# Taps on column tiles of the array: two convolutions of a four-block vision kernel

## The chip, the cores and the metric

The kernel runs on one core of a Trainium2 chip. The metric is the device time of one execution in microseconds (us); the time before is the median of three runs. A core has five engines with their own instruction streams: TensorE (PE, with its weight loads listed as PEld), VectorE (DVE), ScalarE (ACT), GpSimd (POOL) and SyncE (SP), which here only issues transfers. They wait for each other by semaphores.

## The reference, cut to what matters

The input is 16 images of 96 channels and 16 x 16 pixels. Four blocks follow each other, and each is a mixer and a feed-forward, both on a normalised x and added to x.

```python
# mixer of block 0: every channel by itself
out = bn_l(dwconv(x, w_large, 13x13)) + bn_s(dwconv(x, w_small, 3x3)) + bn_i(x)
# mixer of block 1: linear projections, softmax attention of 6 heads
# mixer of block 2: v, q at full size, k, off at stride 2, all depthwise 3x3
value, query = dwconv(x, w_v) + b_v, dwconv(x, w_q) + b_q
key, off     = dwconv(x, w_k, stride 2) + b_k, dwconv(x, w_off1, stride 2) + b_off1
o   = gelu(layernorm(off) * ln_g + ln_b)
pos = tanh(o @ w_off2 + ref_points)
v_sampled = bilinear_sample(value, pos)             # 64 points an image
out = (query . key * scale) @ v_sampled             # 12 heads, no softmax
y   = out @ w_out
# mixer of block 3: depthwise 3x3 q, k, v, and an attention
# feed-forwards of blocks 0 to 2: four experts, two of them weighted for each pixel
h = gelu(x @ w1[e] + b1[e]);  y = sum over e of gate[e] * (h @ w2[e] + b2[e])
# feed-forward of block 3: sign weights; outputs scaled by the largest value of a group
z = bitlinear(x, W1, b1)   # 5 groups; clip(a * 128 / (max|a| + eps), +-(128 - eps))
h = gelu(z);  y = bitlinear(h, W2, b2)
```

## The kernel before

X lies in SBUF as 32 tiles of 128 pixels x 96 channels for the whole time, and each block adds to it. Everything is float32, and each float32 product is two PE instructions in the trace. Each of the eight parts is a function with one block of five engine streams, written out by hand in the order in which they run, with semaphores between them.

`l0_conv` (lines 208 to 407) takes 12 groups of 8 channels. A group's pixels are turned by two PE transposes (line 373) so that the 128 partitions are 8 channels x 16 columns x of the image; ScalarE copies them to `xt` (line 295). A row of taps r of the 13 is then one 128 x 128 band matrix, block diagonal over the channels, which ScalarE fills from `band` by eight strided copies for three groups at a time (`fill`, line 287). `conv_group` (line 388) adds 13 products into PSUM, each with the image rows that its shift leaves. `turn_back` (line 397) turns the result into pixels, and VectorE adds it to X (line 355). The BN factors are 36 powers on GpSimd (line 267), beside the two sets of 16 for the normalisation (line 272).

`moe` (lines 847 to 1129) is the expert feed-forward; the class `ExpertFront` (lines 457 to 550) holds its first steps, which for block 0 stand at the head of `moe`: statistics and root, apply, `pe_turn` (line 540), the copies to a high and a low part, the weight splits, `pe_gates` (line 547). The first product of the experts is at line 1081.

`l2_conv` takes eight pairs of images (`p`), and one pass of its loop holds the first half of pair p and the second half of pair p - 1. `third_xp` is the padded transposed image (96 channels on the partitions), double buffered. `conv` (line 1886) makes a depthwise 3x3 of nine products, each with a 96 x 96 diagonal matrix from `third_diag` and a shifted view. It serves the offsets (`conv_offsets`), the keys and the queries; the values are made by VectorE with nine taps (`value_taps`, line 1718; the first by ScalarE). `scores` (line 1936) multiplies queries and the keys that GpSimd spread over heads (`kb`, line 1650); `sample` (line 1947), `outputs` (line 1957) and `project` (line 1966) finish a pair. In `outputs` a product has 64 x 32 tiles at three column positions. The class `ThirdFront` makes the first normalised tiles and the diagonal inside the expert block before.

The order of TensorE in one pass:

```python
conv_offsets(p); project(p - 2, 1); scores(p - 1, 0); scores(p - 1, 1)
turn_offsets(p); conv_keys(p); turn_values(p - 1)
conv_queries(p, 0, 4); sample(p - 1, 0); turn_back(p)
conv_queries(p, 4, 7); sample(p - 1, 1); positions(p)
conv_queries(p, 7, TAPS); outputs(p - 1, 0); turn(p + 1)
outputs(p - 1, 1); project(p - 1, 0)
```

`l3_ffn` takes five groups of six tiles (768 pixels). For a group: `turn`, `ups` (three chunks of 512 pixels, then three of 256), the maximum over the whole group (`top_in`, `top_out`), `factors` and `clip` on VectorE (line 2483), `gelus` on ScalarE (line 2562), `downs` (line 2611), `results`, `add_results`. `add_term` (GpSimd, line 2407) and `scale_term` (ScalarE, line 2533) add the last value term of the attention to X, `rstd_of` (line 2412) makes the root in three batches, one group and one group and then two, and `stay_awake` (line 67) puts products of the identity with itself on TensorE.

## Time and profile before

| | us |
|---|---|
| median of three runs | 1257.62 |
| lowest and highest run | 1248.44, 1257.85 |
| profiled execution, its own time | 1257.45 |
| span of that execution in the trace | 1255.6 |
| granted TensorE clock, mean | 0.968 |

The span is the time from the first to the last recorded instruction; the profiled execution is 1.85 us longer. A clock of 1.00 is 2.4 GHz, and 0.5 is 1.2 GHz. A row of the timeline is a run of like instructions: its start, the time from the first start to the last end, engine, line, operation, tiles, count, and in brackets how long the engine had been idle and what it waited for. "PE" rows can overlap the next row, since the last instruction's end is counted in.

### The profile page before, as it was taken

The page shows a single profiled execution, that of the slowest core. Times are in us where ns is not written, and L with a number is a line of the kernel's source. Part 1 is how long each engine was busy: PE and PEld are TensorE (multiplying, and loading weights), DVE is VectorE, ACT ScalarE, POOL GpSimd, SP SyncE. Part 2 cuts the span into 40 slices and gives each one's busy share as a digit, 9 for nine tenths or more (in the row PEclk, how much of TensorE's full clock was granted, in tenths as well). Part 3 has the DMA queues.
Part 4 walks back from the last instruction along what each step waited for, and adds up shares of the span by engine and source line. Part 5 has one row for each costly group of instructions (what it writes and reads, how often), then busy time and mean ns, then how long its engine had stood idle before and what let it go on. Part 6 is the DMA issues. An engine that isn't in the chain of part 4 may idle for free. (4 is left out here: it accounts for less than half of the span.)

```text
span 1255.6 us, 24199 instructions
## 1 busy us (share of the span) xinstructions
PE 1170.9 (93%) x8554; PEld 1023.1 (81%) x8554; DVE 807.0 (64%) x2909; ACT 482.4 (38%) x942; POOL 255.6 (20%) x239
## 2 busy tenths in 40 slices
PE   1989999989999999999999999999999999999776
PEld 1978999978999998999997767678999987887555
DVE  6036767666766653778775656655877767776645
ACT  3614434325555553434342232233334322332542
POOL 4003121220110001321222422342121222111200
PEclk9998999998999998999999999999999999999786
DMA  3301001010000000000000000000000000000000
GB/s 137 88 2 66 23 1 49 1 51 1 1 2 1 2 1 1 2 1 0 0 1 1 2 1 2 1 1 1 2 1 0 0 1 1 1 1 4 1 10 38
DMA packets 11563, 15.70 MB, mean 13 GB/s; under 512 B 7385, under 2 KB 9007, under 8 KB 11346
## 3 DMA queue, kind: packets, MB, share of 16 engines
q1 hardware_dynamic: 10754, 12.86, 3.2%
q10 hardware_dynamic: 720, 1.66, 0.3%
q8 instruction: 55, 0.90, 0.3%
q14 instruction: 34, 0.28, 0.1%
HBM read 11.37 MB, written 3.15 MB: 12 GB/s over the span
## 5 line engine op out<-in xcount | busy, mean ns | idle before, releaser
L1091 PEld LDWEIGHTS moe_dn<-all_w,moe_hid 128*128 128x128 f32 x2304 | 269.8, 192 | 5.5
L1091 PE MATMUL moe_dn<-all_w,moe_hid 128*128 128x96 f32 x2304 | 271.8, 275 | 0.0
L1024 ACT ACTIVATE moe_hid<-moe_up 128x512 f32<-128x512 f32 x288 | 169.9, 598 | 232.3 <-PE moe_up L1083 219.3
L1081 PE MATMUL moe_up<-front_xh,front_w1h 97*128 97x512 f32 x288 | 122.4, 425 | 0.6 <-PEq L1141 0.3
L1083 PE MATMUL moe_up<-front_xl,front_w1h 97*128 97x512 f32 x288 | 114.4, 397 | 0.0
L1082 PE MATMUL moe_up<-front_xh,front_w1l 97*128 97x512 f32 x288 | 113.6, 394 | 0.0
L969 DVE SCALAR_TENSOR_TENSOR all_X<-moe_dn,front_gate,all_X 128x96 f32 (+1 forms) x384 | 95.4, 310 | 26.0 <-PE moe_dn L1091 20.3
L961 DVE SCALAR_TENSOR_TENSOR all_X<-all_b,front_gate,all_X 128x96 f32 (+1 forms) x384 | 100.9, 324 | 5.8 <-DVE front_var L83 2.8
L916 POOL TENSOR_TENSOR front_prob<-front_euler,front_logit 128x16 f32<-128x16 f32 x21 | 60.9, 2902 | 190.6 <-DVEq L424 190.6
L1477 PE MATMUL l1c_o<-second_vs,l1c_pt 128*128 128x64 f32 x768 | 92.8, 274 | 0.4 <-DVE l1c_ro L1287 0.4
L1477 PEld LDWEIGHTS l1c_o<-second_vs,l1c_pt 128*128 128x128 f32 x768 | 90.2, 192 | 2.8 <-issue 0.6
L1253 DVE TENSOR_REDUCE second_nmax<-l1c_sc 128x2 f32<-128x512 f32 x96 | 61.8, 686 | 37.6 <-PE l1c_sc L1446 36.6
L1718 DVE SCALAR_TENSOR_TENSOR l2c_val<-third_xp,all_l_taps,l2c_val 96x544 f32<-96x544 f32 x64 | 65.2, 1019 | 13.6 <-ACT l2c_val L1794 11.0
L2159 DVE SCALAR_TENSOR_TENSOR l3c_ykv<-fourth_xp,all_l_taps,l3c_ykv 96x256 f32<-96x256 f32 x128 | 65.1, 508 | 4.0
L1886 PE MATMUL l2c_qp<-third_xp,third_diag 96*96 96x512 f32 x144 | 65.8, 592 | 0.0
L1083 PEld LDWEIGHTS moe_up<-front_xl,front_w1h 97*128 97x128 f32 x288 | 54.7, 190 | 12.7
L2283 PE MATMUL l3c_qp<-fourth_xp,fourth_wqt 96*128 96x256 f32 x288 | 64.8, 378 | 0.0
L1376 ACT ACTIVATE l1c_pt<-l1c_st 128x512 f32<-128x512 f32 x96 | 52.1, 595 | 32.6 <-PE l1c_st L1462 31.5
L1081 PEld LDWEIGHTS moe_up<-front_xh,front_w1h 97*128 97x128 f32 x288 | 55.3, 192 | 9.4 <-issue 1.0
L1082 PEld LDWEIGHTS moe_up<-front_xh,front_w1l 97*128 97x128 f32 x288 | 55.3, 192 | 8.8
L2283 PEld LDWEIGHTS l3c_qp<-fourth_xp,fourth_wqt 96*128 96x128 f32 x288 | 53.2, 189 | 6.9
L388 PE MATMUL l0c_cp<-l0c_xt,l0c_full 128*128 128x176 f32 (+6 forms) x312 | 56.0, 336 | 0.0
(418 smaller groups left out, 2017.5 us busy)
## 6 DMA issues: line engine op xcount, KB each, us to landing
all_w<-w SPq DMA_DIRECT2D x3, 582.0 KB
all_w<-w SPq DMA_DIRECT2D x3, 576.0 KB
all_X<-x_rows SPq DMA_DIRECT2D x2, 768.0 KB, 6.9
conv_scratch<-all_X SPq DMA_DIRECT2D x2, 768.0 KB, 3.2
all_X<-conv_scratch SPq DMA_DIRECT2D x2, 768.0 KB, 4.9
out_tokens<-l3f_y SPq DMA_DIRECT2D x5, 288.0 KB, 2.1
l0c_band<-band ACTq DMA_DIRECT2D x1, 1248.0 KB, 9.4
all_b<-b SPq DMA_DIRECT2D x3, 192.0 KB
```

Of the source, the lines that this page charges most:

```text
L961: last = dve.scalar_tensor_tensor(out=x, in0=b2[:, e, :], scalar=gate[:, p, j, e:e + 1], in1=x, op0=ALU.mult, op1=ALU.add)
L969: last = dve.scalar_tensor_tensor(out=x, in0=dn[e % 2][:, j * C:(j + 1) * C], scalar=gate[:, p, j, e:e + 1], in1=x, op0=ALU.mult, op1=ALU.add)
L1024: act.activation(hid[:, n, :], up[n % UPS][:, :], ACT.Gelu).then_inc(hid_done, 1)
L1081: pe.matmul(bank, w1h[:, n, :], xh[:, p, :], start=True, stop=False)
L1082: pe.matmul(bank, w1l[:, n, :], xh[:, p, :], start=False, stop=False)
L1083: pe.matmul(bank, w1h[:, n, :], xl[:, p, :], start=False, stop=True).then_inc(up_done, 1)
L1091: last = pe.matmul(dn[e % 2][:, j * C:(j + 1) * C], hid[:, n, j * P:(j + 1) * P], w2[:, n, :], start=(k == 0), stop=(k == KC - 1))
L1477: last = pe.matmul(o_ps[:, at:at + VWIDE], pt[:, 2 * (n % 2) + i, m * PIX + t * P:m * PIX + (t + 1) * P], vs[:, b % RV, m, h * VW:h * VW + ...
L1718: ins = dve.scalar_tensor_tensor(out=v, in0=image, scalar=taps[:, 3, t:t + 1], in1=v, op0=ALU.mult, op1=ALU.add)
L1886: ins = pe.matmul(o, diag[:, w, t, :], images(p)[:, :, dy:dy + SIDE:stride, dx:dx + SIDE:stride], start=(t == 0), stop=(t == TAPS - 1))
L2159: ins = dve.scalar_tensor_tensor(out=y3, in0=image, scalar=taps[:, 1, t:t + 1], in1=y3, op0=ALU.mult, op1=ALU.add)
L2283: ins = pe.matmul(o, wqt[:, t, :], xp[:, b % 2, dy:dy + SIDE, dx:dx + SIDE], start=(t == 0), stop=(t == TAPS - 1))
```

## The change

1. **`l0_conv`.** The contraction takes two image rows: 64 partitions hold 4 channels x 16 columns of row r, 64 hold the same of row r + 1. A product has a 128 x 64 weight, and the two halves of a group's channels go to output partitions 0 to 63 and 64 to 127. The 13 rows of taps become 7 pairs. The turns become products with the identity onto 64-wide positions, `fill` fills one group of a ring of six by four copies, `xt` is written by two copies for each group. The BN factors are made for three groups first and for nine groups behind the two normalisation roots, and are spread to the new layout by small products (`spread_factors`). The last two groups run in halves of eight images (14 pieces).
2. **`ExpertFront` of block 0** moves into `l0_conv`: weight splits and constants beside its pieces, statistics, apply, turn and copies at its end. The scaling of the block 1 weights moves from VectorE to GpSimd in `moe(0)`.
3. **`l2_conv`.** The 3x3 of 32 channels is three products (one for each dx) over 96 rows: three copies of the 32 channels, shifted by one image row each, which nine transfers within SBUF make for each pair (`stack`). The three channel groups use 32-wide column positions. `turn(p + 1)` and `tokens_out(p + 1)` move behind `scores`, `normalise` runs one pair earlier.
4. **`l3_ffn`.** `add_term`, `scale_term` and the fillers go. VectorE adds and makes statistics group by group (`group_sums`), GpSimd makes one root for each group, `add_results` runs one pass earlier, the turn stands behind `top_out`. `l3_conv` adds the term of group 1 (`add_m0(TG, 2 * TG)`) at its end.

The diff, cut to its core:

```diff
-                    last = pe.matmul(out[:, :, lo:hi], full[:, g * KL + r, :, :].rearrange("p c x -> p (c x)"),
-                                     xt[:, g, :, lo + d:hi + d], start=(n == 0), stop=(n == KL - 1))
+                for m, j in enumerate(order):
+                    d = 2 * j - KL // 2
+                    lo, hi = max(0, -d - 1), min(SIDE, SIDE - d)
+                    for a, rows in enumerate((LOWER, UPPER)):
+                        out = cp[g % 2][rows, 0:PIX].rearrange("p (i r) -> p i r", r=SIDE)
+                        last = pe.matmul(out[:, images, lo:hi], full[:, g % RF, a, j, :, :].rearrange("p c x -> p (c x)"),
+                                         xt[:, 2 * g + a, images, lo + d + 1:hi + d + 1],
+                                         start=(m == 0), stop=(m == PAIRS - 1))
...
+            for n in range(NP):
+                conv_piece(n)
+                if n + 2 < NG:
+                    turn(n + 2)
+                if n >= 1:
+                    turn_back(n - 1)
...
+            F.pe_turn(pe)
+            turn_back(NP - 1)
...
+    def stack(self, sp, p, stacked):
+        for g in range(SG):
+            for r in range(KS):
+                sp.dma_start(self.st[DH * r:DH * (r + 1), p % 2, g, 0:PAD + SIDE, :],
+                             self.xp[DH * g:DH * (g + 1), p % 2, r:r + PAD + SIDE, :]).then_inc(stacked, 16)
...
+            for p in range(1, NP):
+                wait(sp, S["xp_done"], p + 1)
+                wait(sp, S["q_in"], p - 1)
+                B.stack(sp, p, stacked)
...
-                for t in range(lo, hi):
-                    dy, dx = t // KS, t % KS
-                    ins = pe.matmul(o, diag[:, w, t, :], images(p)[:, :, dy:dy + SIDE:stride, dx:dx + SIDE:stride],
-                                    start=(t == 0), stop=(t == TAPS - 1))
+                for dx in range(lo, hi):
+                    for g in range(SG):
+                        ins = pe.matmul(o[DH * g:DH * (g + 1)], wst[:, w, KS * g + dx, :],
+                                        stacks(p)[:, g, :, 0:SIDE:stride, dx:dx + SIDE:stride],
+                                        start=(dx == 0), stop=(dx == KS - 1))
...
-                wait(act, S["q_in"], p - 1)
+                wait(act, stacked, EACH * (p - 1))
...
             def conv_offsets(p):
-                wait(pe, S["xp_done"], p + 1)
+                wait(pe, stacked, EACH * (p + 1))
...
+            def group_sums(g):
+                lo, hi = TG * g, TG * (g + 1)
+                if g > 1:
+                    chain.sync(dve.scalar_tensor_tensor(out=X[:, lo:hi, :], in0=kv[:, lo:hi, VW], scalar=m0[:, 0:1],
+                                                        in1=X[:, lo:hi, :], op0=ALU.mult, op1=ALU.add))
                 for n in range(lo, hi):
                     last = dve.bn_stats(N["stats"][:, n, :], X[:, n, :])
...
                 if i + 1 < QG:
                     ups(i + 1)
-                    stay_awake(pe, tp[1], ident, 4)
-                if i + 2 < QG:
-                    turn(i + 2)
                 downs(i, 0)
                 top_in(i + 1)
                 downs(i, 1)
                 top_out(i + 1)
+                if i + 2 < QG:
+                    turn(i + 2)
                 downs(i, 2)
```

## Rows read from the trace of the kernel before

**Rows 1.** The page: busy time of the engines, share of the span, instructions.
```profile
PE 1170.9 (93%) x8554; PEld 1023.1 (81%) x8554; DVE 807.0 (64%) x2909; ACT 482.4 (38%) x942; POOL 255.6 (20%) x239
```

**Rows 2.** Windows: stretch, length, busy by engine, clock, DMA share, GB/s.
```profile
30.90:88.70 57.80, 57.35 (x339) 55.64 (x338) 9.98 (x34) 23.47 (x39) 0.00 (x0) 1.00 0.17 48
88.70:106.10 17.40, 9.34 (x28) 7.51 (x29) 10.38 (x48) 8.65 (x14) 6.36 (x11) 0.61 0.15 52
669.10:685.80 16.70, 15.23 (x64) 9.82 (x64) 10.73 (x21) 4.96 (x12) 5.31 (x5) 0.90 0.00 0
...
798.20:820.60 22.40, 22.40 (x206) 16.07 (x205) 13.38 (x27) 6.61 (x17) 6.67 (x8) 1.00 0.01 2
...
1170.00:1256.00 86.00, 62.20 (x311) 47.65 (x310) 46.45 (x130) 35.08 (x71) 2.49 (x2) 0.76 0.05 18
```

**Rows 3.** Timeline, TensorE, the first two groups of the first convolution.
```profile
30.87 9.30 PE L388 MATMUL l0c_cp<-l0c_xt,l0c_full 128*128 128x256 f32 x52
```

**Rows 4.** Timeline, the roots at its start and TensorE at its end.
```profile
6.14 6.13 POOL L267 TENSOR_TENSOR l0c_inv<-l0c_shift,l0c_mhalf 128x36 f32<-128x36 f32 x1 [5.29 <-DVEq L315]
...
12.24 6.28 POOL L272 TENSOR_TENSOR l0c_rstd<-l0c_var,l0c_mhalf 128x16 f32<-128x16 f32 x2
...
87.43 0.38 PE L397 MATMUL l0c_bp<-all_ident,l0c_conv 128*128 128x128 f32 x2
...
99.52 0.77 PE L1081 MATMUL moe_up<-front_xh,front_w1h 97*128 97x512 f32 x1
```

**Rows 5.** Timeline, TensorE, one pair of the third convolution.
```profile
798.27 2.49 PE L1886 MATMUL l2c_fp<-third_xp,third_diag 96*96 96x128 f32 x18
...
801.11 3.01 PE L1936 MATMUL l2c_mix<-l2c_q,l2c_kb 96*64 96x64 f32 x48
...
806.86 3.60 PE L1886 MATMUL l2c_qp<-third_xp,third_diag 96*96 96x512 f32 x8
...
816.70 1.88 PE L1886 MATMUL l2c_qp<-third_xp,third_diag 96*96 96x512 f32 x4
818.51 0.64 PE L1957 MATMUL l2c_mix<-l2c_at,l2c_vbt 64*32 64x64 f32 x24
```

**Rows 6.** Timeline, VectorE and ScalarE in the same pair.
```profile
799.02 3.25 DVE L1718 SCALAR_TENSOR_TENSOR l2c_val<-third_xp,all_l_taps,l2c_val 96x544 f32<-96x544 f32 x4 [0.19 <-ACT l2c_val L1794]
...
804.40 0.27 DVE L1702 BATCH_NORM_STATS2 l2c_ostats<-l2c_fp 128x6 f32<-128x96 f32 x1 [1.73 <-PE l2c_fp L1909]
...
807.54 4.45 DVE L1718 SCALAR_TENSOR_TENSOR l2c_val<-third_xp,all_l_taps,l2c_val 96x544 f32<-96x544 f32 x3
811.96 0.55 DVE L1734 TENSOR_TENSOR l2c_vbt<-l2c_vb,all_l_mask 64x384 f32<-64x384 f32 x1
...
816.90 0.38 ACT L1823 ACTIVATE l2c_th<-l2c_fp 128x256 f32<-128x256 f32 x1 [4.24 <-PE l2c_fp L1918]
...
818.76 0.67 ACT L1811 ACTIVATE l2c_q<-l2c_qp,all_l_bias 96x512 f32<-96x512 f32 x1
```

**Rows 7.** SyncE's queue: one issue (timeline), and landing times (the page).
```profile
39.62 0.43 SPq L133 DMA_DIRECT2D all_l_wqk<-l_wqk  x1
...
all_X<-x_rows SPq DMA_DIRECT2D x2, 768.0 KB, 6.9
...
out_tokens<-l3f_y SPq DMA_DIRECT2D x5, 288.0 KB, 2.1
```

**Rows 8.** Timeline of the last feed-forward: up products and the long root.
```profile
1164.20 3.66 PE L2603 MATMUL l3f_up<-l_xt,all_l_w 97*128 97x256 f32 x6 [2.74 <-ACT l3f_hid L2554]
...
1190.20 2.34 PE L2603 MATMUL l3f_up<-l_xt,all_l_w 97*128 97x512 f32 x6
...
1192.64 2.27 POOL L2412 TENSOR_TENSOR l_rstd<-l_var,l_mhalf 128x12 f32<-128x12 f32 x1 [22.81 <-DVE l_shift L2440]
...
1198.03 3.78 PE L2603 MATMUL l3f_up<-l_xt,all_l_w 97*128 97x256 f32 x6 [5.49 <-ACT l3f_hid L2554]
...
1208.25 2.34 PE L2603 MATMUL l3f_up<-l_xt,all_l_w 97*128 97x512 f32 x6
```

More of the change, by code:

```diff
@@ L280, in _ @@
             act.dma_start(own[:, :], A["own"]).then_inc(w_in, 16)
-            def fill(chunk):
-                groups = slice(chunk * FG, (chunk + 1) * FG)
-                rows = slice(chunk * FG * KL, (chunk + 1) * FG * KL)
-                for k in range(GC):
-                    last = act.activation(full[:, rows, k, :], band[:, groups, :, :].rearrange("p g r x -> p (g r) x"),
-                                          ACT.Copy, scale=own[:, k:k + 1])
-                last.then_inc(full_done, 1)
@@ L307, in _, with fill @@
-            work.act_signs(act)
+            def fill(g):
+                act.wait_ge(band_done, 1 if g < FIRST else 2)
+                if g >= RF:
+                    act.wait_ge(conv_done, g - RF + 1)
+                for k in range(HC):
+                    last = act.activation(full[:, g % RF, :, :, k, :].rearrange("p a j x -> p (a j) x"),
+                                          band[:, 2 * g:2 * g + 2, :, :].rearrange("p a j x -> p (a j) x"), ACT.Copy,
+                                          scale=own[:, k:k + 1])
+                last.then_inc(full_done, 1)
@@ L351, in _, with normalise @@
[L351 to L357 removed]
+            def normalise(c):
+                lo, hi = CHUNKS[c], CHUNKS[c + 1]
+                for h, half in enumerate(halves):
+                    wide = lambda a: a[:, half].unsqueeze(1).broadcast_to([P, hi - lo, SIDE])
+                    if c == 0:
+                        dve.wait_ge(ln_rstd, h + 1)
+                    out = xn[:, h, lo:hi, :]
+                    chain.sync(dve.tensor_tensor(out, x0[:, half, lo:hi].rearrange("p t c -> p c t"), wide(mean),
+                                                 ALU.subtract))
+                    last = dve.tensor_tensor(out, out, wide(rstd), ALU.mult)
+                last.then_inc(xn_done, 1)
@@ new lines, in turn @@
+            def turn(g):
+                pe.wait_ge(xn_done, next(c for c in range(len(CHUNKS)) if CHUNKS[c] >= GC * (g + 1)))
+                if g >= 2:
+                    pe.wait_ge(xt_done, g - 1)
+                for a in range(2):
+                    for h in range(2):
+                        x = xn[:, h, GC * g + HC * a:GC * g + HC * (a + 1), :].rearrange("p c x -> p (c x)")
+                        for rows in (LOWER, UPPER):
+                            last = pe.matmul(tp[g % 2][rows, (2 * a + h) * P:(2 * a + h + 1) * P], x, ident[:, :],
+                                             start=True, stop=True)
+                last.then_inc(turned, 1)
@@ L894, in _ @@
                         reread_half(sp, T, h)
+        if layer == 1:
+            @block.sync
+            def _(sp):
+                follow.sp_tokens(sp)
         @block.gpsimd
@@ L1980, in _ @@
                     scores(p - 1, 1)
+                if live(p + 1):
+                    turn(p + 1)
                 if live(p):
```

474 lines of the change are left out of this document (259 added, 215 removed).

## The prediction

> **What bounds the kernel now.** I read the page first: TensorE is busy 93% of a span of 1255.6 us and VectorE 64% [rows 1], so a change pays where it shortens TensorE's own work, or the stretches in which TensorE waits. Then the windows over the stretches that the diff touches [rows 2]. In the first convolution (30.9 to 88.7) TensorE works 57.35 of 57.8 us and VectorE only 9.98. In one pair of images of the third convolution (798.2 to 820.6) it works 22.40 of 22.40, VectorE 13.38, ScalarE 6.61, GpSimd 6.67. Both are bound by TensorE. Two stretches are not: the hand-over to the first expert block (88.7 to 106.1, 9.34 of 17.40, granted clock 0.61, which is a mix of 1.2 and 2.4 GHz), and the last feed-forward (1170 to 1256, 62.20 of 86, clock 0.76). The timelines give the single terms.
>
> **First convolution.** Before, a group of eight channels is 26 instructions in 4.65 us (52 in 9.30), [rows 3]. Its 13 products have 2656 columns, so a column costs 1.75 ns. After, a group has seven products for each half of its output, with 16 x (11+13+15+16+14+12+10) = 1456 columns, and the two halves stand on two column positions of the array. If these run side by side, the products take 1456 x 1.75 ns = 2.55 us, otherwise 5.10. The row for this is in the third convolution: its small products on three column positions, 24 instructions of 64 columns, take 0.64 us from first start to last end, while 48 such instructions on one position take 3.01 [rows 5]. That is 27 ns against 63 for each, and with the last one's own duration taken off it is nearer to three at once. I take side by side.
>
> The turns into pixel layout become eight products of 128 columns on 64-wide positions: four deep, 4 x 128 x 1.75 ns = 0.90 us. The turn back stays two transposes, about 0.24 of the 0.38 that the row at 87.43 gives with the last one's own length [rows 4]. TensorE must twice change between narrow and full width. Eight full-width instructions take 3.60, with 0.59 for the last one alone, so their starts are 0.43 apart; the four from 816.70 would end their turn at 818.42, and the narrow ones start at 818.51 [rows 5]: 0.1 a change, 0.2 a group. Sum 2.55 + 0.90 + 0.24 + 0.2 = 3.9 us a group. The ten full pieces make 39, the four half pieces (1.27 + 0.12 + 0.2) 6.4. ScalarE has four copies of 224 elements, two of 512 and one of 256 for each group; a copy of 512 takes 0.67 [rows 6], so about 3 us a group: under 3.9, covered, but with little to spare. Without the cover (the pieces with weight splits and constants beside them) I add 1 us once.
>
> Start: GpSimd takes 6.13 us for 36 roots and 3.14 for 16 [rows 4], so about 0.7 + 0.15 for each element. Its order is now 9 (2.1 us, from 6.1), 16, 16 (the second starts when its variances are there, about 13.5, until 16.7), 27 (4.7, until 21.4). The products wait for it, since the spreading of the factors stands ahead of them on TensorE: first product at 22.2 instead of 30.87. End of the pieces: 22.2 + 39 + 6.4 + 1 = 68.6; before, 87.4. What follows up to the expert products (99.52) takes 12.1 us [rows 4]. The expert front's statistics, weight splits and constants now lie beside the pieces, but statistics of X need the last add-back, and then roots, apply, turn, copies and the gate products still follow one another: I keep 9.5 us of it. First expert product at 78 instead of 99.5: **-21.5 us**; the range of this term is -12 (ScalarE binds at 4.7 a group) to -26. The cold start of the expert products stays.
>
> The Trainium skill says (TensorEngine Tiling (Array Packing), on column tiling) that tiles work independently, and that a change of tiling mode drains the array. The trace agrees on both, with 0.64 us for 24 and about 0.1 for a change; by its rule the sum is the same.
>
> **Third convolution.** The taps of a convolution stay nine products of two instructions, but three stand on three column positions: the 18 instructions of 128 columns (2.49 us) go to about 0.85, and the 18 of 512 columns (8 of them 3.60, so 8.1) to 2.7 [rows 5]. TensorE's work in a pair falls by 2 x 1.6 + 5.4 = 8.6 with the first and last ends taken off, less 0.6 for six more changes of width: from 22.4 to about 14.4. Now the others bind. One turn of the chain that returns to itself, from the project product: conv_offsets with two changes 1.0, the second project 0.5, scores 2.95 [rows 5], turn 0.6, turn_offsets 0.15, that is 5.2; then VectorE from the offsets' moments at 804.40 to the end of sampled_out at 811.96 + 0.55, 8.1 [rows 6], which holds three taps at 1.48 each while GpSimd's kb runs beside them, against 3.25 / 4 = 0.81 where it doesn't; sample 1.4; positions 0.5; ScalarE from tanh at 816.90 to the end of q at 818.76 + 0.67, 2.5; outputs_out 0.4. Sum 18.1, and 18.2 with small gaps. The four taps of the next value lie beside scores. So a pair takes 18.2 instead of 22.45, 4.25 less: seven times that is 29.8. The first pair (16.7 us, [rows 2]) has no samples beside it and loses 5.5. The last step with the expert front's logits gives back 1.5. **-34 us.** TensorE now idles 3.8 us in a pair in two or three gaps. Bounds: if only TensorE binds, 14.6 a pair, -60; if the gaps make the clock fall to 1.2 GHz for a third of the work, that is 4.8 us more work, of which the gaps take up about half: +2.5 a pair, -16.
>
> The stacks: nine transfers of 78 KB a pair on SyncE's queue. An issue costs 0.43 us there, and 288 KB from SBUF land in 2.1 [rows 7]. tokens_out moves behind scores, to about 5.8 us into the step; + 0.6 + 9 x 0.43 + 2.1 = 12.4, 5.8 us before conv_offsets of the next pair. Costed at nothing; above 11.8 us from the copy to landing, it binds. The queue holds nothing else there. For the first pair the transfers go out in the expert block, under its last products. tokens_out now waits for the stacks of two pairs back, long landed.
>
> **Last feed-forward.** What goes: GpSimd's four additions and ScalarE's scaling at the start, and the 12-element root (2.27 us) with its copy of six tiles behind it, for which the second half of the up products of group 2 waits 5.49 us; in group 0 that wait is 2.74 [rows 8]. In their place VectorE does the addition and statistics group by group: 0.8 + 1.1 + 1.3 = 3.2 us in each of three groups, behind clip. The start gains about 5. A steady group: before, ups(2) and ups(3) start 18.05 us apart, with the 5.49 in it [rows 8]. In its place the maxima wait until VectorE is through with add_results (1.4) and the sums (3.2), about 2 us of wait by the timeline's order, so 3.5 less; eight fillers less, 1.2; and since the turn stands behind top_out, ups waits for gelu and copy, 0.9 more: 14.2, and about 12.6 in the groups without sums. The two other distances before are 16.2 and 15.5: 2 + 3.8 + 2.9 = 8.7. With the start 13.7. The fillers also kept TensorE busy: I take back 4 for a lower clock, the clock being 0.76 already. **-10 us**, bounds +3 and -15. The added add_m0 in the block before (0.8) is covered by the fillers that stand at its end.
>
> **Sum.** 1255.6 - 21.5 - 34 - 10 = 1190.1. The profiled execution took 1257.45 us (span 1255.6), the median is 1257.62: 2 us on top, **1192 us**.
>
> **Rivals.** (a) TensorE stays the bound of the third convolution: the taps on VectorE overlap other work and GpSimd's kb moves off them. For it speaks the slack that a planner would find (VectorE 13.4 of 22.4 busy), against it that moments, taps, sampled_out, positions and copies depend on each other. At 15.5 a pair 19 less: 1173. (b) The clock: TensorE had no gap in the pairs before and has 3.8 us now, and in the last feed-forward, with waits up to 5.49 us, it averages 0.76 [rows 2, 8]. With a fall in each pair, +2.5 x 7, and 5 more at the end: 1214. (c) The stacks are late: nine transfers of 2.1 each, one after the other, are 19 us and 25.4 with the copy: the pair becomes 25.4, 7 x 7.2 = 50 more: 1242. (All nine carry 705 KB, and the 768 KB of one half of the input take 6.9 [rows 7].) It decides from 11.8 us; against it, the transfers go to separate places and the queues are empty (2 GB/s in a pair, [rows 2]). (d) The wide column tiles do not run side by side, because their 96 or 128 rows and 128 to 512 columns are not the 64 rows and 64 columns of the row measured. Then a group of the first convolution takes 5.10 + 1.8 + 0.24 + 0.2 = 7.3, 2.6 more, over 12 groups +31; the third convolution gains nothing and pays 0.6 a pair, +5; the start (-8.7), the hand-over (-2.5) and the feed-forward (-10) stay: +15, 1272, slower. It decides if more than about two thirds of the overlap is missing. The Trainium skill (TensorEngine Tiling (Array Packing)) names no such limit of size; no row here shows tiles of 96 rows side by side.
>
> **Chances.** The forecast 0.50 (1180 to 1203 by itself); (a) 0.16; (b) 0.22; (c) 0.05; (d) 0.03; the rest, other mishaps in the hand-over, 0.04. Range 1165 to 1222 leaves out (c), (d), and the ends of (a) and (b). Of faster by more than 1%, within 1% and slower by more than 1% (1% is about what a measurement of this kernel can tell from no change), faster has all but (d) and half of the rest and of (c): 0.93; same 0.04; slower 0.03.
>
> **What would show it.** A run of 28 product instructions in 2.5 to 2.6 us on L0's pieces, the pieces 3.9 apart, the first near 22 us; expert products from 78. In the third convolution 18.2 us a pair with TensorE near 14.5 busy, VectorE's moments and taps following one another without idle, conv_offsets released by VectorE's or ScalarE's side and not by a DMA. In the last part no wait on GpSimd, starts of ups 14 and then under 13 us apart. The prediction is wrong if conv_offsets waits for a transfer, if the granted clock in the pairs is under 0.9, or if ScalarE sets the pace of the first convolution.

## The result, and the profile after

| | before | changed |
|---|---|---|
| median, us | 1255.04 | 1206.43 |
| lowest and highest | 1248.44, 1257.85 | 1203.24, 1213.95 |
| span of the profiled execution | 1255.6 | 1207.0 |
| granted TensorE clock, mean | 0.968 | 0.952 |

The kernel before ran once more beside the changed one, so its median here is of four runs. The ratio of the changed kernel to the one before is 0.9629, with a 95% interval of 0.9564 to 0.9693: faster by 3.7%, 48.6 us. The forecast was 1192 in 1165 to 1222. So the time lies within the range, and a quarter of the expected 65 us of gain is missing. (The kernel before varies: beside the experiments its medians were 1251.0 to 1256.0 us, and its profiled execution, with 1257.45 us, is one of the longest. A stage difference below is one profiled execution against one.) The two profiled spans differ by 48.6 us as well, and they divide as follows. (A stage runs from its first product to the first of the next. The second and the fourth line hold stretches that the diff hardly touches.)

| stage, us | before | changed | difference | forecast |
|---|---|---|---|---|
| start to first expert product | 99.5 | 85.7 | -13.8 | -21.5 |
| experts, block 1, experts | 569.6 | 571.3 | +1.6 | 0 |
| third convolution | 188.8 | 165.1 | -23.7 | -34 |
| experts, fourth mixer | 301.1 | 301.1 | 0 | 0 |
| last feed-forward | 96.5 | 83.8 | -12.7 | -10 |

The page of the changed kernel, busy time and share of the span (against [rows 1]), then windows over the same stretches as [rows 2] (length, busy time of TensorE, its weight loads, VectorE, ScalarE, GpSimd, granted clock, DMA share, GB/s):

```profile
PE 1111.6 (92%) x8774; PEld 967.2 (80%) x8774; DVE 810.0 (67%) x2904; ACT 485.6 (40%) x976; POOL 255.7 (21%) x244
```

```profile
23.40:63.70 40.30, 38.82 (x466) 30.36 (x462) 13.99 (x23) 34.14 (x78) 0.00 (x0) 1.00 0.27 76
63.70:80.60 16.90, 10.12 (x120) 8.78 (x119) 9.95 (x42) 4.86 (x11) 1.37 (x1) 0.79 0.00 1
657.00:822.00 165.00, 142.03 (x1652) 102.66 (x1652) 110.16 (x258) 51.59 (x125) 64.84 (x59) 0.87 0.13 31
1123.10:1207.00 83.90, 61.23 (x292) 43.50 (x292) 55.31 (x167) 38.05 (x77) 6.08 (x8) 0.82 0.05 18
```

The third convolution used to run at a clock of 1.00, with TensorE busy all the time, from its second pair on [rows 2, 5]. Now the clock is 0.87 there, which is about 43 of 165 us at 1.2 GHz. That is the first thing that the page shows and the sum had not priced.

The timeline of TensorE in the first convolution of the changed kernel, which answers to [rows 3, 4]:

```profile
23.42 2.73 PE L487 MATMUL l0c_cp<-l0c_xt,l0c_full 128*64 128x256 f32 x28
25.98 1.04 PE L468 MATMUL l0c_tp<-all_ident,l0c_xn 128*64 128x128 f32 x16
...
36.18 2.73 PE L487 MATMUL l0c_cp<-l0c_xt,l0c_full 128*64 128x256 f32 x28
...
40.09 2.77 PE L487 MATMUL l0c_cp<-l0c_xt,l0c_full 128*64 128x256 f32 x28
...
63.29 0.44 PE L498 MATMUL l0c_bp<-all_ident,l0c_conv 128*128 128x128 f32 x2
67.17 0.60 PE L171 MATMUL l0c_tp<-l0c_rs,l0c_ones 128*128 128x10 f32 x2 [3.45 <-DVEq L166]
67.70 2.70 PE L487 MATMUL l0c_cp<-l0c_xt,l0c_full 128*64 128x128 f32 x28
...
73.83 1.50 PE L487 MATMUL l0c_cp<-l0c_xt,l0c_full 128*64 128x128 f32 x28
...
85.73 0.77 PE L1212 MATMUL moe_up<-front_xh,front_w1h 97*128 97x512 f32 x1
```

The 28 product instructions of a piece take 2.7 us with the last one's own length, and from the fourth on the pieces stand 3.93 us apart (the 16 instructions of the turns take about 1.0): the sum's 2.55, 0.90 and 3.9. Between 63.7 and 67.2 TensorE waits 3.45 us for VectorE. Line 171 is `pe_means`, the product for the means of the last block's weights. In the stream it comes right behind a piece. VectorE first does that piece's add-back, from 63.76 us, and then the sums, until 67.07; only then can the product start. Behind this wait the first two half pieces take 2.70 us each at half the clock, and the last two, at full clock, 1.50.

One pair of the third convolution, at a clock of 0.99, as windows over all pairs and as a timeline of the pair from 748.6 (TensorE, then VectorE, the stack transfers and ScalarE; against [rows 5, 6]):

```profile
668.50:687.20 18.70, 16.99 (x203) 12.52 (x197) 12.44 (x37) 7.44 (x18) 6.26 (x7) 0.84 0.16 39
687.20:709.07 21.87, 21.00 (x206) 15.30 (x205) 13.90 (x26) 6.17 (x16) 12.09 (x12) 0.69 0.14 33
709.07:728.56 19.49, 16.60 (x205) 11.90 (x204) 14.36 (x36) 6.57 (x17) 7.33 (x8) 0.91 0.16 38
728.56:748.60 20.04, 16.62 (x205) 11.68 (x204) 15.03 (x33) 6.57 (x17) 8.90 (x9) 0.91 0.16 37
748.60:767.00 18.40, 15.26 (x205) 10.89 (x204) 12.99 (x27) 6.80 (x17) 7.56 (x8) 0.99 0.17 40
767.00:787.90 20.90, 17.78 (x205) 13.16 (x204) 12.13 (x23) 6.33 (x17) 6.61 (x8) 0.85 0.15 35
```

```profile
748.61 0.96 PE L2024 MATMUL l2c_fp<-third_st,third_wst 96*32 96x128 f32 x18
...
750.11 3.01 PE L2075 MATMUL l2c_mix<-l2c_q,l2c_kb 96*64 96x64 f32 x48
...
754.36 6.10 SPq L833 DMA_DIRECT2D third_st<-third_xp  x9
...
756.65 3.89 DVE L1857 SCALAR_TENSOR_TENSOR l2c_val<-third_xp,all_l_taps,l2c_val 96x544 f32<-96x544 f32 x3
...
760.45 0.54 DVE L1873 TENSOR_TENSOR l2c_vbt<-l2c_vb,all_l_mask 64x384 f32<-64x384 f32 x1
...
761.14 1.51 PE L2086 MATMUL l2c_vb<-l2c_vt,l2c_bil 128*64 128x96 f32 x16 [1.57 <-DVE l2c_vbt L1873]
...
766.18 0.91 PE L2105 MATMUL l2c_ky<-all_l_wout,l2c_oc 96*128 96x96 f32 x4 [0.87 <-ACT l2c_oc L1984]
```

The clock column and the length go together but for the first row, whose 18.70 us at 0.84 hold fewer waits: 18.40 us at 0.99, 19.49 and 20.04 at 0.91, 20.90 at 0.85, 21.87 at 0.69. The 18 instructions of the offsets' taps take 0.96 us instead of 2.49. TensorE's waits are where the chain had them: 1.57 us for VectorE's first copy, which stands behind three taps, and 0.87 us for ScalarE's output copy.

The up products of the second, fourth and fifth group in the last feed-forward (against [rows 8]):

```profile
1133.36 6.74 PE L2712 MATMUL l3f_up<-l_xt,all_l_w 97*128 97x512 f32 x12 [1.36 <-ACT l_xt L2663]
...
1161.85 2.42 PE L2712 MATMUL l3f_up<-l_xt,all_l_w 97*128 97x512 f32 x6 [1.21 <-ACT l_xt L2663]
...
1175.83 4.53 PE L2712 MATMUL l3f_up<-l_xt,all_l_w 97*128 97x512 f32 x12 [0.88 <-ACT l_xt L2663]
```

### The profile page after: what moved, and what is told of

It is laid out like the page before. It is cut to its first block and busy times, and to the rows that moved or that the text cites. A ratio compares the mean times of both kernels' runs of the same rounds, so it can differ in the third digit from the quotient of the medians.

```text
span 1207.0 us, 24782 instructions
## 1 busy us (share of the span) xinstructions
PE 1111.6 (92%) x8774; PEld 967.2 (80%) x8774; DVE 810.0 (67%) x2904; ACT 485.6 (40%) x976; POOL 255.7 (21%) x244
## 5 line engine op out<-in xcount | busy, mean ns | idle before, releaser
L1056 POOL TENSOR_TENSOR front_rstd<-front_var,front_mhalf 128x4 f32<-128x4 f32 x21 | 21.3, 1015 | 129.6 <-DVEq L1082 129.2
L2086 PEld LDWEIGHTS l2c_vb<-l2c_vt,l2c_bil 128*64 128x64 f32 x256 | 24.8, 152 | 27.7 <-issue 27.7
```

## Experiments

All are the changed kernel with one edit, unless it is said otherwise. A filler is a product of the identity with itself (two instructions) that only keeps TensorE busy. A pair is one pass of the third convolution's loop. "L0" is the time of the first expert product, "third" the length of the third convolution, "ffn" that of the last feed-forward, each of the profiled execution; the median and the ratio to the kernel before are of all runs. The changed kernel itself has L0 85.7, third 165.1, ffn 83.8, median 1206.4, ratio 0.9629.

| run | L0 | third | ffn | median | ratio, 95% interval |
|---|---|---|---|---|---|
| e1_means_later | 80.6 | 167.8 | 83.8 | 1209.1 | 0.9649, 0.9605 to 0.9692 |
| e2_fillers_l2 | 84.6 | 165.8 | 87.0 | 1209.0 | 0.9632, 0.9578 to 0.9687 |
| e3_group_major | 85.7 | 173.1 | 85.7 | 1212.6 | 0.9683, 0.9634 to 0.9732 |
| e4_sampled_early | 84.7 | 173.8 | 83.9 | 1211.8 | 0.9636, 0.9585 to 0.9686 |
| e5_no_stacks | 84.9 | 164.8 | 83.9 | 1207.7 | 0.9658, 0.9595 to 0.9722 |
| e6_half_major | 106.0 | 167.8 | 83.7 | 1230.5 | 0.9825, 0.9779 to 0.9871 |
| e7_ffn_fillers | 85.2 | 164.7 | 79.6 | 1202.2 | 0.9583, 0.9540 to 0.9626 |
| e8_three_together | 83.0 | 156.0 | 82.8 | 1195.8 | 0.9554, 0.9524 to 0.9585 |
| e9_ffn_alone | 99.8 | 188.8 | 83.2 | 1243.3 | 0.9925, 0.9900 to 0.9950 |
| e10_fewer_fillers | 82.2 | 156.2 | 83.0 | 1193.1 | 0.9510, 0.9469 to 0.9552 |
| e12_all | 82.9 | 151.4 | 79.8 | 1187.7 | 0.9493, 0.9472 to 0.9513 |
| e11_all_tail | 81.2 | 153.1 | 79.4 | 1188.7 | 0.9495, 0.9463 to 0.9526 |

### Do narrow products run side by side? e3_group_major and e6_half_major

```diff
-                for dx in range(lo, hi):
-                    for g in range(SG):
+                for g in range(SG):
+                    for dx in range(lo, hi):
```

> Changed kernel, with the products of the third convolution's taps ordered by channel group first and by dx second, so that three (in the queries, one) products follow each other on one column position, instead of one on each of the three in turn. Same products, same number. Theory: the gain comes from products side by side on different column positions, and neighbours in the stream must be on different ones. Offsets and keys go from 0.96 us to about 2.3 (18 instructions of 128 columns), the queries stay at 1.06 since a part has one dx; a pair gets about 2.5 us longer, 18 to 20 us in all. Rival: the array sorts them by itself, nothing changes. Rival: the 0.96 us is no overlap but a cheaper narrow product: nothing changes either, and the queries tell nothing.

The timeline of TensorE in this kernel, at a pair at full clock:

```profile
729.63 1.47 PE L2024 MATMUL l2c_fp<-third_st,third_wst 96*32 96x128 f32 x18
...
735.24 1.47 PE L2024 MATMUL l2c_ky<-third_st,third_wst 96*32 96x128 f32 x18
```

```diff
-                for m, j in enumerate(order):
-                    for a, rows in enumerate((LOWER, UPPER)):
+                for a, rows in enumerate((LOWER, UPPER)):
+                    for m, j in enumerate(order):
```

> Changed kernel, with the products of the first convolution ordered by half first (seven for the lower 64 output partitions, then seven for the upper) instead of in turn. Same products. Theory: the two halves then run one after the other, 28 instructions take 5.1 us instead of 2.7, a piece 6.4 instead of 3.93, twelve groups 28 us more: first expert product at 112 instead of 85.7, the median at 1233 to 1236. Rival: a 64-wide product is cheaper than a 128-wide one of as many columns: nothing changes.

The same view of the first convolution in this kernel: one piece in the middle, the start of the next, and a half piece at full clock. The rows alternate, since products of the next turn start between the last ones of the piece:

```profile
34.07 4.24 PE L487 MATMUL l0c_cp<-l0c_xt,l0c_full 128*64 128x256 f32 x25
37.98 0.43 PE L468 MATMUL l0c_tp<-all_ident,l0c_xn 128*64 128x128 f32 x2
38.15 0.47 PE L487 MATMUL l0c_cp<-l0c_xt,l0c_full 128*64 128x192 f32 x2
...
39.93 4.23 PE L487 MATMUL l0c_cp<-l0c_xt,l0c_full 128*64 128x256 f32 x25
...
93.09 2.50 PE L487 MATMUL l0c_cp<-l0c_xt,l0c_full 128*64 128x128 f32 x28
```

Both orders cost time with the same products, so the overlap is real and it depends on neighbours in the stream. In e6 the half pieces take 2.50 us in place of 1.50, which is "one after the other" (2 x 1.27). The full pieces come 5.85 us apart in place of 3.93 (6.4 expected), and the first expert product 20 us later in place of 28 (the 1.48 us for which TensorE waits for ScalarE once, ahead of 35.8 us in the changed kernel, went as well). In e3 the 18 instructions take 1.47 us, between 0.96 and the 2.3 expected.

The starts of the single instructions in the two traces tell why both fall short of the expectation. In the half piece at 95.77 us of e6, the lengths of the instructions tell the two halves of the output apart: the first instruction of the second half starts at 96.789, 6 ns behind the 11th of the 14 of the first half, and the other three of the first half follow beside it. In e3 the third instruction starts at 729.881 and the fourth at 729.887, and from there the starts fall into three rows of six. This fits three positions, each begun 0.26 us after the one before. Within a row they are 113 to 142 ns apart, as in the changed kernel with three side by side (113 to 144) and as at full width before (113 to 150). So a product for a busy position waits, and one for a free position, a few places behind it in the stream, goes ahead. Two thirds of the three positions' overlap survive in e3 for this reason. The rival "the narrow product is merely cheaper" falls: the order alone changes the time, and on one position the narrow products start no closer than wide ones.

e3's whole is 6 us slower in its two runs, with intervals that overlap. Its profile puts 8 us into the third convolution, though the clock was at 1.2 GHz for 44 us of it in both kernels; pairs at full clock take 19.3, 19.5 and 18.7 us against 18.4. Twice the 0.5 us by which 18 instructions got longer would be 1.0.

### What makes the first convolution's end slow? e1_means_later

```diff
-                if n == NG - 3:
+                if n == NG - 2:
                     work.pe_means(pe)
...
-                if n == NG - 3:
+                if n == NG - 2:
                     work.dve_centre(dve, chain)
```

> Changed kernel, with the product for the weight means (pe_means) and what VectorE makes of it (dve_centre) one piece of the first convolution later. Theory: the 3.45 us for which TensorE waits at 63.7 us for VectorE's sums (dve_sums) is what made the granted clock fall over the next two half pieces (2.70 us each, against 1.50 at full clock). Then both go: no wait of over 1 us between the pieces, half pieces at 1.5 us, first expert product at 79.5 to 80.5 instead of 85.7, the median about 5 us less (1201). Rival: the clock falls there anyway (narrow tiles count less, or the turn-backs' small gaps do it): the wait goes, the half pieces stay at 2.7, first expert product at 82.3. Rival: the late sums only move the wait one piece on: 85.7 as before.

The timeline of TensorE there:

```profile
67.40 1.49 PE L487 MATMUL l0c_cp<-l0c_xt,l0c_full 128*64 128x128 f32 x28
...
69.08 1.50 PE L487 MATMUL l0c_cp<-l0c_xt,l0c_full 128*64 128x128 f32 x28
```

In this execution all half pieces take 1.5 us and the first expert product comes at 80.6, 5.1 us earlier: the theory's number. A wait of 1.3 us for ScalarE's copy shows in place of the 3.45. The median doesn't show it (1209.1, and the interval holds the changed kernel's ratio). In this profile the third convolution is 2.7 us longer, and the spread between executions (1203 to 1214 for the changed kernel) is larger than the effect. What a stage gains here has to be read from the stage.

But one execution isn't enough for that either. e8, e10 and e12 have the same edit in this stage and nothing else there, and TensorE's waits are the same 1.3 and 0.3 us. Yet the clock fell for 3.4 us over their half pieces, and the first expert product comes at 82.2 to 83.0. The timeline of TensorE in e8:

```profile
68.01 0.39 PE L171 MATMUL l0c_tp<-l0c_rs,l0c_ones 128*128 128x10 f32 x2 [0.29 <-DVEq L166]
68.33 1.97 PE L487 MATMUL l0c_cp<-l0c_xt,l0c_full 128*64 128x128 f32 x28
...
70.64 2.40 PE L487 MATMUL l0c_cp<-l0c_xt,l0c_full 128*64 128x128 f32 x28
```

That is the expectation's first rival (82.3). The kernels without the edit have 84.5 to 85.7, and the changed kernel's profile is at the upper end, with 6.8 us at 1.2 GHz there (e2, e4, e5 and e7 have 3.4). So the long wait is gone in every run with the edit; that its going keeps the clock up isn't shown. The edit is worth about 3 us on the mean of the profiles, between 1.5 and 5.

### Do the stack transfers cost anything? e5_no_stacks

```diff
-            for p in range(1, NP):
+            for p in range(1, 2):
...
-                wait(act, stacked, EACH * (p - 1))
+                wait(act, stacked, EACH * min(p - 1, 2))
...
-                wait(pe, stacked, EACH * (p + 1))
+                wait(pe, stacked, EACH * min(p + 1, 2))
```

> Changed kernel without the stack transfers of pairs 2 to 7 (this part is left out; the convolutions read the stacks of pairs 0 and 1 again). Theory: the transfers are hidden (issued from 754.4 to 760.5, needed at 767.0), so a pair stays at 18.4 to 20 us and the whole within 3 us of the changed kernel. Rival: the transfers slow the engines' own accesses to SBUF or hold conv_offsets back: a pair gets over 1 us shorter, 7 us or more in all.

Third convolution 164.8 us against 165.1: nothing. In the changed kernel the nine issues run from 754.36 for 6.1 us and a transfer lands 2.1 us after its issue, by 762.6, while the next pair needs them at 767.0. (The sum had 0.43 us an issue and not 0.68; the slack took that up.)

### Clock or chain in the third convolution? e2_fillers_l2, e4_sampled_early, e8_three_together, e10_fewer_fillers

e2:

```diff
                 if live(p - 1):
+                    fillers(p, 6)
                     sample(p - 1, 1)
...
                     outputs(p - 1, 1)
+                    fillers(p, 3)
                     project(p - 1, 0)
...
+            def fillers(p, count):
+                if live(p + 1):
+                    wait(pe, S["xp_done"], p + 2)
+                    stay_awake(pe, tp, ident, count)
```

> Changed kernel, with products of the identity in the third convolution's waits: six before the second sample product of a pair (12 instructions), three before project (6). Nothing else is changed. Theory: a pair takes 18.4 us at full clock and 19.5 to 21.9 with falls of the clock, which come from TensorE's 3 to 4 idle us. The fillers lie in idle time, so the clock stays at full speed from the third pair on and the pairs take 18.4 to 18.8: 7 to 10 us less in all. Rival: the pairs are long because VectorE and GpSimd delay each other (taps at 1.3 and more instead of 0.81), and the clock is only a by-product: the clock rises, the pairs stay at 19.5 to 20, 0 to 2 us less. Rival: the fillers delay the samples by their own length: 1 us more in a pair, 7 us more.

Windows of this kernel: a pair with fillers, and the stretch behind the last of them (the same columns as above).

```profile
705.50:723.70 18.20, 17.46 (x226) 12.90 (x226) 14.40 (x36) 6.58 (x17) 7.36 (x8) 1.00 0.17 41
...
798.10:820.40 22.30, 19.62 (x157) 17.96 (x157) 3.13 (x8) 1.41 (x4) 1.24 (x4) 0.50 0.00 1
```

Where the fillers stand, the clock is 1.00 from the third pair on, and the pairs from the second on take 20.2, 19.3, 18.2, 18.9, 18.2 and 18.2 us. (The second begins while the clock is still low. The third and the fifth have a second wait of 0.8 to 0.9 us at full clock, which I did not follow up.) So the theory holds for the pairs. But the last two passes have no fillers, and there the clock fell for 27 us: the stretch from the last full pair to the next block is 41.4 us, against 34.2. The whole gained nothing. The fillers' own length lay in idle time: a pair with them is as long as the fastest without.

e4:

```diff
                 if live(p):
-                    value_taps(p, 6, TAPS)
+                    value_taps(p, 6, 7)
                 if live(p - 1):
                     sampled_out(p - 1, 0)
+                if live(p):
+                    value_taps(p, 7, TAPS)
```

> Changed kernel, with VectorE's sampled_out(p - 1, 0) behind the first of the last three value taps instead of behind all three. Theory: the chain that sets a pair goes through these taps (the second sample product waits 1.6 to 2.3 us for that copy), so TensorE's wait there goes and a pair gets 1.2 to 2 us shorter, 17 us at full clock; over seven pairs 8 to 14 us less, 1194 to 1200. Rival: VectorE's own sum of work and its second copy (behind normalise) is what outputs waits for, so the wait only moves to outputs: 0 to 3 us less in all. Rival: the clock sets the pairs: no change beyond 2 us.

Windows and the timeline of TensorE in this kernel:

```profile
701.80:723.70 21.90, 21.02 (x210) 15.24 (x205) 13.20 (x37) 6.61 (x18) 7.26 (x8) 0.68 0.14 34
723.70:743.20 19.50, 17.95 (x210) 13.40 (x207) 14.29 (x33) 6.53 (x18) 9.24 (x9) 0.83 0.16 38
```

```profile
725.95 4.95 PE L2077 MATMUL l2c_mix<-l2c_q,l2c_kb 96*64 96x64 f32 x48
...
737.29 1.53 PE L2088 MATMUL l2c_vb<-l2c_vt,l2c_bil 128*64 128x96 f32 x16
```

The wait ahead of the second sample product is gone (no bracket at 737.29), as the theory had it. The stage is nevertheless 8.7 us longer, since the clock is at 0.68 and 0.83. The 48 instructions of scores, which always lie on the chain, take 4.95 us instead of 3.01. A shorter chain by itself was worth nothing here. It also says something of the clock. No wait of TensorE in these pairs is above 0.9 us, and they come to about 1.5 us a pair, half of the changed kernel's; yet the clock was at 1.2 GHz for 89 us of the stage, against 44. In part that is because slow work fills the waits. But the pair from 663.7, slow only in its first 5 us, has waits of 0.8 and 0.9 us, and the clock fell right behind it, at 682.5. So fewer and shorter waits alone did not hold it up.

e8 (the fillers of e2, in its last pass too, with e1 and e4):

> Changed kernel with three edits together: the weight means one piece later (e1), fillers in the third convolution's waits (e2, and in its last pass too), sampled_out(p - 1, 0) behind one of the three taps (e4). Theory: alone, the shorter chain of e4 was eaten by the clock, which was at 1.2 GHz for 88 us of that stretch; with fillers it stays up, and the pairs take 17 us or less, against 18.2 with fillers alone. First expert product at 80, third convolution in 147 to 152 us instead of 165, whole 1185 to 1192. Rival: the fillers take up what the shorter chain gives, or VectorE's work per pair (13 to 15 us with contention) and the second copy bind: pairs stay at 18.2, whole 1193 to 1198.

The third convolution takes 156.0 us, 9 less, and the whole is 10.6 us below the changed kernel (the intervals still overlap by 0.002). The second and third pair take 20.1 and 19.2 us and the four behind them 18.1 each, as with the fillers alone. That is the expectation's rival. The reason is in the timeline of TensorE:

```profile
749.64 1.07 PE L2026 MATMUL l2c_qp<-third_st,third_wst 96*32 96x512 f32 x6
750.64 1.60 PE L67 MATMUL l2c_tp<-all_ident 128*128 128x128 f32 x12
752.17 1.53 PE L2088 MATMUL l2c_vb<-l2c_vt,l2c_bil 128*64 128x96 f32 x16
```

The sample product starts right behind the fillers: they fill, and partly cause, the whole gap that the earlier copy had opened.

e10, its edit against e8:

```diff
-                    fillers(p, 6)
+                    fillers(p, 2)
                     sample(p - 1, 1)
...
+                if p == 0:
+                    fillers(p, 8)
                 if live(p):
                     turn_back(p)
                     conv_queries(p, 1, 2)
+                if p == 0:
+                    fillers(p, 2)
```

> The kernel with three edits (e8), with two fillers instead of six before the second sample product, and ten in the first pair, where TensorE idles. Theory: six fillers (1.6 us) fill exactly the wait that the earlier copy had opened, since TensorE has no idle time there in e8; with two the pairs take 17.0 to 17.3 us instead of 18.1 (TensorE's own work with the fillers left is 16.3), the clock stays up, and the first two pairs are 3 us shorter: the third convolution takes 143 to 148 us instead of 156. Rival: another wait (the second copy, or ScalarE's q and the output copies) then shows in front of outputs or project, and the pairs stay at 18. Rival: too few fillers, the clock falls again: 19 and more in single pairs.

Windows: a pair of this kernel, and its last stretch.

```profile
718.30:735.50 17.20, 16.49 (x215) 11.98 (x214) 13.84 (x33) 6.56 (x17) 9.21 (x8) 1.00 0.18 42
787.70:807.70 20.00, 18.06 (x167) 16.43 (x167) 3.08 (x8) 1.40 (x4) 1.18 (x4) 0.66 0.00 1
```

17.2 us for each of the last four full pairs, 0.9 below e8 and 1.0 below e2: the earlier copy pays when the clock is held and the fillers leave it room (the two were not separated). The stage stays at 156.2. 5 of the missing 8 us and more against the expected 143 to 148 are a fall of the clock behind the last filled pair (0.66 over 20 us), after a pass without fillers; in e8 the same pass had none either, and the clock stayed at 1.00. The rest lies in the first pairs, which came out 0.3 us shorter together and not 3.

### The last feed-forward: e9_ffn_alone and e7_ffn_fillers

e9 is the kernel before with the changed `l3_ffn` and the added `add_m0(TG, 2 * TG)`.

> Kernel before, with the last mixer's end and the last feed-forward of the changed kernel (add_m0(TG, 2 * TG), group_sums and all that goes with them) and nothing else. Theory: this part gives 12.7 us of the 48.6 by itself, whatever stands ahead of it: the stretch from the first up product to the end goes from 96.5 to 83.8 us, the whole to 1243. Rival: part of it comes from the state in which the stages before leave the clock: then 5 to 9 us.

That stretch takes 83.2 us, against 96.5 before and 83.8 in the changed kernel, and with its old neighbours it is as long as with the new ones: what stands ahead of it makes no difference. The median of 1243.3 hits the expected 1243, but by luck. That number was worked out from the long profiled execution, and the kernel before had a median of 1251.0 beside this run. So the whole gained 7.7 us (ratio 0.9925; the interval is 6 to 12.5 us), not 12.7. The profiled execution of the kernel before had a clock of 0.968 and a span of 1255.6 us; e9 has 0.973, and executions of the kernel before at 0.973 have spans of 1249 to 1251. If that difference lies in this stretch, which at a clock of 0.77 has more than half of the time at 1.2 GHz, it usually took some 6 us less than 96.5. Only one trace of the kernel before was kept, so this stays open; 7.7 us is what the medians show.

e7:

```diff
                     turn(i + 2)
                 downs(i, 2)
+                if i + 1 < QG:
+                    wait(pe, S["up_out"], MS * (i + 2))
+                    stay_awake(pe, up[0], ident, 4 if i + 2 < QG else 12)
```

> Changed kernel with fillers in the last feed-forward where TensorE waits 1.4 to 1.5 us ahead of the up products (four, 8 instructions), and twelve in the 3.3 us ahead of the last group's down products, which run at 1.2 GHz (2.9 us for 12 instructions, against 1.58). Theory: the clock there costs 30 us at half speed, of which the tail alone 3 x 1.3 us; with the fillers that stretch goes from 83.8 us to 77 to 80, the whole 4 to 7 us less. Rival: the chain through VectorE sets the end, also in the tail, and the fillers' own length goes on top: 84 or more.

The last group's down products in the changed kernel:

```profile
1189.33 2.53 PE L2720 MATMUL l3f_dn<-all_l_w,l3f_hid 128*128 128x96 f32 x12 [3.34 <-DVEq L2586]
...
1192.31 2.88 PE L2720 MATMUL l3f_dn<-all_l_w,l3f_hid 128*128 128x96 f32 x12
```

and in e7:

```profile
1184.03 2.87 PE L67 MATMUL l3f_up<-all_ident 128*128 128x128 f32 x24
1187.53 1.58 PE L2720 MATMUL l3f_dn<-all_l_w,l3f_hid 128*128 128x96 f32 x12 [0.63 <-DVEq L2586]
```

83.8 to 79.6 us, 4.2 less. The median is 4.3 us lower; its interval still overlaps with that of the changed kernel, so it is the stage that shows it. These waits are not where the removed fillers stood, so this doesn't show that removing those was wrong; it shows that fillers in the new waits pay.

### A faster version: e12_all and e11_all_tail

e12 has the edits of e10 and e7, six fillers ahead of the second sample product in the last two passes (in the first of them into a bank that scores no longer needs), and three ahead of project in the pass that had none.

> The edits of e10 and e7 together (weight means later, earlier copy, two fillers ahead of the second sample product, three ahead of project, fillers in the last feed-forward), and six fillers ahead of the second sample product also in the last two passes, after which the clock fell for 13.7 us in e10. Theory: stages add: third convolution 148 to 150 us (156 less the fall), last feed-forward 79.6, whole 1180 to 1186. Rival: the clock that one stage saves another loses, since it falls by the stages' order: 1189 or more.

A window over the whole third convolution of this kernel:

```profile
652.50:804.00 151.50, 141.44 (x1769) 104.07 (x1769) 106.41 (x259) 51.63 (x125) 65.82 (x61) 0.98 0.15 34
```

1187.7 us, ratio 0.9493 with an interval of 0.9472 to 0.9513, below the whole interval of the changed kernel: 19 us less than it and 64 less than before. The stages add, as the theory said; the median is 2 us above its range, the third convolution 1.4 above. e11, its edit against e12:

```diff
+            pe.wait_ge(conv_out, NP)
+            stay_awake(pe, cp[0], ident, 12)
             F.pe_turn(pe)
```

> As e12, with twelve fillers ahead of the expert front's turn at the end of the first convolution, where TensorE waits 3.4 us. Theory: of the expert products behind it, 12 run at 1.2 GHz in 0.43 us each instead of 0.23; with the fillers the clock stays up and the first up products save 2 to 4 us. Rival: the wait of 2.2 us at the boundary of the two blocks, which can't be filled, is enough for the fall: no change beyond 1 us. Rival: the add-back of the last half piece is behind the fillers: 0 to 1 us more.

The first expert product comes 1.7 us earlier in this profile, the median is the same (1188.7). Whether those fillers help can't be said from this.

## Why the prediction was right in direction and too large

The range was met, the forecast's own band (1180 to 1203) was not, by 3 us. The stages missed by +7.7, +10.3, +1.6 and -2.7 us, so a little of the closeness is luck. One of the signs that the prediction had named for being wrong came true: the granted clock in the pairs is under 0.9 in three of the seven windows, and 0.87 over the stage. What happened is the forecast with part of rival (b) on it, and (b) by itself would have given 1214.

**Narrow products side by side** (2.55 us for a group, 0.85 for a convolution at stride 2): right, 2.7 and 0.96 with the last one's own length. The rivals (c), late stacks, and (d), no overlap at this size, are excluded, by e5 and by e3 and e6. The change of width was priced at 0.1 us; pieces of 3.93 us against 3.9 leave no room for more.

**First convolution** (-21.5, measured -13.8). The start is 1.2 us late (23.42, not 22.2), and the ten full pieces take 1.3 us more than 39, with one wait of 1.48 us for ScalarE's copy. The step that failed is the end of the pieces, "6.4 + 1", where 1 us stood for the pieces with the weight work beside them. From 63.7 to 77.0 they took 13.3 us, 5.9 more. That work has a product on TensorE's own queue, and I didn't ask what it waits for once the pieces are 3.93 instead of 4.65 us: 3.45 us of wait, and 2.4 us for two half pieces at 1.2 GHz behind it. What follows up to the expert products, put at 9.5 us, took 8.7. With the product one piece later, e1, e8, e10 and e12 give 1.5 to 5 of the 7.7 us back.

**Third convolution** (-34, measured -23.7). The chain was right: 18.2 us forecast, 18.40 measured at full clock, 5.1 saved in the first pair (5.5 forecast). The failed term is the clock. It stood in the text as rival (b) with 2.5 us a pair and a chance of 0.22, and not in the sum. It cost 1.6 us a pair on the mean of 20.0 over the seven. e2 and e8 show that it is the clock and not the chain: where it is held at 1.00, most pairs take 18.1 to 18.2 us. What lets it fall is shown less well. The idle that I had named, 3.8 us in a pair (3.1 measured), came with it, but e4 had half of that idle and twice the time at 1.2 GHz. The pairs also differ from those before in their narrow products, and the fillers are both work in a wait and full-width products. No run separates the two. The prediction's own rows had a hint, since the stretches below a clock of 1.00 in [rows 2] are those with idle time.

**Experts, block 1, experts** (+1.6, forecast 0). The code there is all but the same. The changed kernel has its falls of the clock at other places; the experiments have 567 to 572 us for this stretch, so it is within what it varies by.

**Last feed-forward** (-10, measured -12.7). The start gained 4.7 (the second up products at 1133.4, 10.2 us behind the first ones, against 14.9), and the waits for the long root went, as forecast. The next groups start 13.8, 14.7 and 14.0 us apart; the last was forecast under 13. I took 4 us off for a lower clock; over the whole stretch the clock rose instead, from 0.77 to 0.82. That the waits that were cut were longer than the fillers that left may be the reason, but no run shows it. The time before is that of a long execution, and by the medians of e9 this part gives 7.7 us: the forecast of 10 lies between the two. Fillers in the new waits are worth 4.2 us more (e7).

**Rival (a)**, TensorE as the bound at 15.5 us a pair: excluded as it stood, since TensorE is busy 15.3 of 18.4 us. With fillers and the earlier copy the pairs come to 17.2.

## What to carry to other kernels

When a change takes work away from the engine that was never idle, price the clock together with the chain: here pairs with 3 us of waits in 18 took 20.0 us on the mean and not 18.2. Put cheap products into the waits up to the end of the stretch, no more than the wait is long, and look at the passes after the last one, for that is where the clock fell next. An edit that shortens the chain can look worthless (e4) until the clock is held (e10). A stage read from one execution can mislead too: e1 showed 5 us, and three kernels with the same edit 1.5 to 3.5. And when one engine's pieces get shorter, go through every foreign instruction on its queue and ask whether its producer still is in time.

## What the runs showed of the hardware

The column positions of TensorE overlap by the order of the stream: 18 instructions of 96 rows and 128 columns take 0.96 us when neighbours alternate over three positions, and 1.47 us grouped, with 2.49 us for as many full-width ones before. 28 instructions on two 64-wide positions take 1.50 us in turn and 2.50 grouped. The start of a product is not held to the order of the stream: in e6 products for the free half started 6 ns behind the 11th of 14 for the busy half.

The granted clock fell to 1.2 GHz in pairs whose longest wait on TensorE was 2.3 us, in e4 in pairs without a wait above 0.9 us. It held at 1.00 in pairs with fillers that had one wait of 0.7 us, and in e8 and e10 also in one with two waits of 0.8 and 0.9. Where it falls is not fixed: in e7, whose third convolution is the changed kernel's, the pairs from the second on take 18.4, 21.3, 21.0, 20.3, 19.6 and 18.2 us, in the changed kernel 18.7, 21.9, 19.5, 20.0, 18.4 and 20.9. So a stage gain of 5 us can vanish in a median, as in e1.
